# Graph layer kernel: the node stage's result stores are issued by SyncE instead of GpSimd, ahead of the segment loads

## The chip, the cores and the metric

One core of a Trainium2 chip. The metric is the time of one execution on the device, in microseconds; the median of the runs counts.

## The reference

50,000 nodes with 128 features, 50,000 edges sorted by target node, 32 edge types, weights built from 8 bases.

```python
h = jnp.maximum(_layernorm(x, axis=-1), 0.0)
W_rel = jnp.einsum('rb,bdf->rdf', w_comp, weight)
seg = etype * n_nodes + dst
agg = jax.ops.segment_sum(h[src] * norm, seg, num_segments=n_rels * n_nodes)
node_repr = jnp.einsum('rnd,rdf->nf', agg.reshape(n_rels, n_nodes, d_in), W_rel)
node_repr = node_repr + h_bias + h @ loop_weight
x = x + jax.nn.relu(node_repr)
```

## The kernel before

Two stages, all in float32. The *message stage* (up to about 770 us) goes over the edges in 98 groups of 4 tiles of 128 edges: GpSimd gathers rows of `x` by indirect DMA, TensorE multiplies them with all 8 bases, ScalarE and VectorE weigh and add the 8 products, and SyncE stores 4 tiles of messages with their target node to the DRAM tensor `msgs` (L332).

The *node stage* goes over the nodes in 98 groups of 4 windows of 128 nodes (`G` = 4; the last group, 97, has two full windows and one of 80 nodes). Since edges are sorted, the messages of a window are consecutive rows of `msgs`. For a group `g`:

- SyncE (SP) waits for the result of group g - 8, loads four row numbers from `row_tab` (L337) and then loads, for each window, 192 rows of messages into `seg` (L341; 96 partitions of 1032 B). A ring of 8 (`LRING`) holds them.
- GpSimd (POOL) waits for the result of group g - 8, stores it (`store_results`, L491; L493 for the 80 nodes), asks for the rows of `x` of group g into `xw` (`load_x`, L498 and L500; also a ring of 8), and works out `rel` of group g - 3, the place of each message's target in its window (L416), once that group's segments have landed. The rows of `x` and `out` that a partition holds are four rows of 128 numbers, 512 B each, which lie 128 rows apart in DRAM.
- VectorE (DVE) takes statistics of `xw` (L943, L957, L963, L968), makes the one-hot matrices `pick` from `rel` (L932), and makes the result: relu of the sums plus `xw`, into `res` (L1086), a ring of 4 (`NRING`). It waits there until the store of group g - 4 has landed (`n_out`), and counts results in `n_res`.
- ScalarE (ACT) normalises into `hw` (L566) and copies the transposes (L574).
- TensorE (PE) transposes `hw` (L718), and for each window adds three products into PSUM: with `w_loop` (L752), and of `pick` with the two halves of `seg` (L753, L755).

On DVE, the step of group g makes the statistics and `pick` of group g + 1 and the result of group g - 2. The order of work on every engine is written out by hand; all loops are unrolled. A branch for unsorted or crowded targets (`compact > 0`) is not taken with these inputs. The order on SP around the change:

```python
def reload_windows(g, n, q, full=G, last=0):

    sp.wait_ge(n_res, g - (LRING - 1))
    load_windows(g, q, row_tab, n_seg[q], full, last)
```

and on DVE:

```python
if not is_before(g, NRING):

    dve.wait_ge(n_out[r], n * (16 * LRING // NRING) + 16 * (q // NRING))
```

Of the kernel before, what the change touches and what calls it, by code (L numbers as in the profile page):

```python
# [27 lines left out]
P = 128  # L28
G = 4
# [5 lines left out]
NRING = 4  # L35
LRING = 8
# [7 lines left out]
def sweep(eng, count, step, ring=RING, peel=5, first=0):  # L44

    for g in range(first, count):
        step(g, g // ring, g % ring)


def hold(eng, passed):  # L50

    eng.sem_inc(passed, 1)


def round_before(n, q, k=1, ring=RING):

    return n + (q - k) // ring
# [27 lines left out]
def build_layer(nc, x, src, dst_cols, dst, dst_next, type_rows, norm, weight, mix_weight, loop_weight, bias, out):  # L85
    N, D = x.shape
# [6 lines left out]
    NW = -(-N // P)  # L93
    LAST = N - (NW - 1) * P
    NGW = -(-NW // G)
# [16 lines left out]
    with ctx:  # L112
        def sb(name, shape, dt=F32):
            return ctx.enter_context(nc.sbuf_tensor(name, shape, dt))
# [4 lines left out]
        def sem(name):  # L119
            return ctx.enter_context(nc.semaphore(name))  # L120
# [83 lines left out]
        res = sb("res", [P, NRING, G, F])  # L204
# [96 lines left out]
        n_res = sem("n_res")  # L301
        n_out = [sem(f"n_out{q}") for q in range(NRING)]

        X_WIN = x[0:(NW - 1) * P, :].rearrange("(w p) d -> p w d", p=P)
        OUT_WIN = out[0:(NW - 1) * P, :].rearrange("(w p) d -> p w d", p=P)
        LAST_FULL = NW - 1 - (NGW - 1) * G
# [3 lines left out]
        @block.sync  # L310
        def _(sp):

            def load_types(c):
                if c >= 2:
                    sp.wait_ge(s_hot, (c - 1) * TYPES)
                groups = min(TYPES, NG - c * TYPES)
                for j in range(G):
                    sp.dma_start(type_bc[R * j:R * j + R, c % 2, 0:groups, :],
                                 type_rows[j:j + 1, c * TYPES:c * TYPES + groups, :].to_broadcast([R, groups, P])
                                 ).then_inc(s_types[c % 2], 16)  # L320

            sp.dma_start(src_all[:, :], src).then_inc(s_src, 16)
            load_types(0)
            sp.dma_start(norm_all[:, :], norm).then_inc(s_norm, 16)
            sp.dma_start(dst_c[:, :], dst_cols).then_inc(s_dst_c, 16)

            def store_messages(g, n, q):
                if g % TYPES == 0 and (g // TYPES + 1) * TYPES < NG:
                    load_types(g // TYPES + 1)
                sp.wait_ge(s_msg, g * G + G)  # L330
                sp.wait_ge(s_dst_col, g + 1)
                sp.dma_start(msgs[g * G * P:(g + 1) * G * P, :].rearrange("(p t) c -> p (t c)", t=G),  # L332
                             msg[:, q, :, :].rearrange("p t c -> p (t c)")).then_inc(s_stored[q], 16)

            def load_windows(g, q, table, done, full=G, last=0):
                windows = full + (last > 0)
                _, rows = nc.values_load_multi_w_load_instructions(  # L337
                    table[0:1, bass.ds(g * G, windows)], (mybir.EngineType.SP,), min_val=0, max_val=ROWS - SEG,
                    skip_runtime_bounds_check_because="first_row is clamped to EP - SEG or counts compacted rows")
                for j, row in enumerate(rows):  # L340
                    sp.dma_start(seg[0:SEG_P, q, j, :, :].rearrange("p c f -> p (c f)"),  # L341
                                 msgs[bass.ds(row, SEG), :].rearrange("(p c) f -> p (c f)", c=CHUNKS)
                                 ).then_inc(done, 16)

            for g in range(NG):
                store_messages(g, g // RING, g % RING)
                if g == MODE_STORE:
                    sp.wait_ge(s_start, 1)
                    sp.dma_start(mode, mode_i[:, :]).then_inc(s_table, 16)
                if g == NG - PREP:  # L350
                    for q in range(RING):
                        sp.wait_ge(s_stored[q], 16 * 4)
                if 0 <= g - (NG - PREP) < LRING:
                    early = g - (NG - PREP)
                    load_windows(early, early, early_tab, n_seg[early])

            sp.wait_ge(s_table, 16)
            compact = sp.value_load(mode, min_val=0, max_val=1)
            for q in range(RING):
                sp.wait_ge(s_stored[q], 16 * len(range(q, NG, RING)))  # L360

            with sp.If(compact > 0):
                with sp.Fori(0, NW + 2) as w:
                    sp.wait_ge(c_zero, w + 1)
                    hold(sp, passed["sp"])
                    sp.dma_start(msgs[bass.ds(w * P + EP, P), :], cz[:, :]).then_inc(c_zero_st, 16)
                with sp.Fori(0, NT) as t:
                    sp.dma_start(cm[:, :], msgs[bass.ds(t * P, P), :]).then_inc(c_load, 16)
                    sp.wait_ge(c_st, t * 16 + 16)
                    hold(sp, passed["sp"])  # L370


                sp.wait_ge(n_rel, EARLY)
                for q in range(LRING):
                    sp.wait_ge(n_seg[q], 16 * G)
                    load_windows(q, q, row_tab, c_reload)

            def reload_windows(g, n, q, full=G, last=0):

                sp.wait_ge(n_res, g - (LRING - 1))  # L380
                load_windows(g, q, row_tab, n_seg[q], full, last)

            sweep(sp, NGW - 1, reload_windows, LRING, LRING, LRING)
            g = NGW - 1
            reload_windows(g, g // LRING, g % LRING, LAST_FULL, LAST)

        @block.gpsimd
        def _(pool):
# [95 lines left out]
                pool.wait_ge(c_pick, EARLY)  # L484


            def store_results(g, q, full=G, last=0):
                r = q % NRING
                pool.wait_ge(n_res, g + 1)
                if full:  # L490
                    pool.dma_start(OUT_WIN[:, bass.ds(g * G, full), :], res[:, r, 0:full, :]).then_inc(n_out[r], 16)  # L491
                if last:
                    pool.dma_start(out[(NW - 1) * P:N, :], res[0:last, r, full, :]).then_inc(n_out[r], 16)  # L493

            def load_x(g, n, q, full=G, last=0):
                store_results(g - LRING, q)
                if full:
                    pool.dma_start(xw[:, q, 0:full, :], X_WIN[:, bass.ds(g * G, full), :]).then_inc(n_x[q], 16)  # L498
                if last:
                    pool.dma_start(xw[0:last, q, full, :], x[(NW - 1) * P:N, :]).then_inc(n_x[q], 16)  # L500
                window_relative(g - LAG, round_before(n, q, LAG, LRING), (q - LAG) % LRING)
# [3 lines left out]
            def window_relative(g, n, q, windows=G):  # L505
                pool.wait_ge(n_seg[q], n * (16 * G) + 16 * windows)
                if not is_before(g, NRING):
                    pool.wait_ge(n_pick, g - (NRING - 1))
                relative(g, n, q, n_rel, windows)

            for g in range(EARLY, LRING - LAG):
                window_relative(g, 0, g)
            sweep(pool, NGW - 1, load_x, LRING, LRING, LRING)
            last_g = NGW - 1
            load_x(last_g, last_g // LRING, last_g % LRING, LAST_FULL, LAST)
            for g in range(NGW - LRING, last_g):
                ahead = g + LRING - LAG
                if ahead < NGW:
                    window_relative(ahead, ahead // LRING, ahead % LRING, G if ahead < last_g else LAST_FULL + 1)
                store_results(g, g % NRING)  # L520
            store_results(last_g, last_g % NRING, LAST_FULL, LAST)
            for r in range(NRING):
                pool.wait_ge(n_out[r], 16 * (len(range(r, NGW, NRING)) + (r == last_g % NRING and LAST_FULL > 0)))

        @block.scalar
        def _(act):
# [635 lines left out]
```

## Time and profile before

| | |
|---|---|
| median of 3 runs | 1082.01 us (1081.96 to 1083.28) |
| profiled execution, its own time | 1083.85 us |
| its span | 1082.1 us |
| mean granted clock of TensorE | 0.995 of 2.4 GHz |
| busy: PE, DVE, ACT, POOL | 97%, 95%, 86%, 75% |
| DMA queues: GpSimd's (q0) | 28224 packets, 76.93 MB, 26.6% of 16 engines |
| SyncE's (q1) | 59682 packets, 71.69 MB, 22.6% |
| ScalarE's (q10, at the start only) | 1664 packets, 0.82 MB, 0.4% |

The profile is of one execution; its rows are in microseconds from the start of the span. Sizes that it gives as KB are of 1024 B. A DMA's share of an instruction on SP, POOL or ACT is its issue alone; the packets are moved by the core's 16 DMA engines, whose mean busy share has its own row. "To landing" is from issue to the last semaphore update. The windows are in time order: the message stage until about 770 us, then the node stage, whose last loads are issued at about 1055 us.

### The profile page before, as it was taken

The page shows a single profiled execution, that of the slowest core. Times are in us where ns is not written, and L with a number is a line of the kernel's source. Part 1 is how long each engine was busy: PE and PEld are TensorE (multiplying, and loading weights), DVE is VectorE, ACT ScalarE, POOL GpSimd, SP SyncE. Part 2 cuts the span into 40 slices and gives each one's busy share as a digit, 9 for nine tenths or more (in the row PEclk, how much of TensorE's full clock was granted, in tenths as well). Part 3 has the DMA queues.
Part 4 walks back from the last instruction along what each step waited for, and adds up shares of the span by engine and source line. Part 5 has one row for each costly group of instructions (what it writes and reads, how often), then busy time and mean ns, then how long its engine had stood idle before and what let it go on. Part 6 is the DMA issues. An engine that isn't in the chain of part 4 may idle for free. (4 is left out here: it accounts for less than half of the span.)

```text
span 1082.1 us, 23544 instructions
## 1 busy us (share of the span) xinstructions
PE 1047.1 (97%) x4903; PEld 665.9 (62%) x4903; DVE 1024.4 (95%) x4361; ACT 932.3 (86%) x3253; POOL 807.6 (75%) x1381
## 2 busy tenths in 40 slices
PE   1999999999999999999999999999899999999997
PEld 0444444444444444444444444444699999999997
DVE  4999999999999999999999999999899999999995
ACT  6899999999999999999999999998588888888884
POOL 5788888888888888888888888886355555555553
PEclk9999999999999999999999999999899999999999
DMA  6122242224223322322244422222499999999993
GB/s 152 47 77 65 75 109 64 76 72 103 74 67 100 84 65 77 99 76 83 75 119 117 134 75 64 77 66 85 129 294 298 292 301 298 298 298 296 295 299 107
DMA packets 89716, 150.96 MB, mean 140 GB/s; under 512 B 18114, under 2 KB 57346, under 8 KB 89570
## 3 DMA queue, kind: packets, MB, share of 16 engines
q0 software_dynamic: 28224, 76.93, 26.6%
q1 hardware_dynamic: 59682, 71.69, 22.6%
q10 hardware_dynamic: 1664, 0.82, 0.4%
q14 instruction: 106, 0.87, 0.3%
q8 instruction: 40, 0.66, 0.3%
HBM read 97.88 MB, written 51.49 MB: 138 GB/s over the span
## 5 line engine op out<-in xcount | busy, mean ns | idle before, releaser
L687 PE MATMUL y_ps<-w_all,hT 128*128 128x512 f32 x1568 | 691.6, 593 | 2.0 <-DVE sum_a L850 1.8
L687 PEld LDWEIGHTS y_ps<-w_all,hT 128*128 128x128 f32 x1568 | 288.7, 190 | 333.0 <-issue 276.9
L442 POOL DMA_INDIRECT xg<-x,idx x392 | 393.5, 1004 | 77.0 <-issue 49.7
L538 ACT ACTIVATE z<-y_ps,mix 128x128 f32<-128x128 f32 x784 | 244.8, 364 | 61.4 <-PE y_ps L687 47.5
L850 DVE SCALAR_TENSOR_TENSOR sum_b<-y_ps,mix,sum_b 128x128 f32<-128x128 f32 x784 | 265.8, 339 | 0.0
L397 POOL TENSOR_TENSOR u<-z 128x128 f32<-128x128 f32 x392 | 181.6, 463 | 38.1 <-ACT z L538 27.4
L491 POOL DMA_DIRECT2D out<-res x98 | 76.1, 777 | 139.8 <-DVE res L1086 139.8
L566 ACT ACTIVATE hw<-xw,shift,nrstd 128x128 f32<-128x128 f32 x392 | 162.1, 482 | 2.0 <-DVE shift L968 0.5
L752 PE MATMUL y_ps<-w_loop,hwT 128*128 128x128 f32 x782 | 152.1, 276 | 0.0
L753 PE MATMUL y_ps<-seg,pick 96*128 96x128 f32 x782 | 152.0, 275 | 0.0
L755 PE MATMUL y_ps<-seg,pick 97*128 97x128 f32 x782 | 151.8, 275 | 0.0
L850 DVE SCALAR_TENSOR_TENSOR sum_b<-y_ps,mix,z 128x128 f32<-128x128 f32 x392 | 136.0, 347 | 14.6 <-ACT z L534 7.4
L534 ACT ACTIVATE z<-y_ps,mix 128x128 f32<-128x128 f32 x392 | 140.4, 358 | 5.7 <-PE y_ps L687 5.3
L596 ACT ACTIVATE h<-xg,neg_mean 128x128 f32<-128x128 f32 x392 | 135.3, 399 | 0.1
L850 DVE SCALAR_TENSOR_TENSOR sum_a<-y_ps,mix,sum_a 128x128 f32<-128x128 f32 x392 | 133.8, 341 | 1.1 <-DVE sum_b L850 1.0
L850 DVE SCALAR_TENSOR_TENSOR sum_a<-y_ps,mix,u 128x128 f32<-128x128 f32 x392 | 133.8, 341 | 0.8 <-POOL u L397 0.7
L752 PEld LDWEIGHTS y_ps<-w_loop,hwT 128*128 128x128 f32 x782 | 119.2, 192 | 0.5 <-issue 0.5
L753 PEld LDWEIGHTS y_ps<-seg,pick 96*128 96x128 f32 x782 | 119.3, 192 | 0.0
L755 PEld LDWEIGHTS y_ps<-seg,pick 97*128 97x128 f32 x782 | 119.1, 192 | 0.0
L932 DVE TENSOR_TENSOR pick<-iota_n,rel 96x1024 f32<-96x1024 f32 (+1 forms) x100 | 118.0, 1180 | 0.0
L883 DVE TENSOR_TENSOR msg<-sum_a,sum_b 128x128 f32<-128x128 f32 x392 | 114.4, 292 | 0.1
L943 DVE BATCH_NORM_STATS2 nstats<-xw 128x6 f32<-128x128 f32 x392 | 89.9, 275 | 0.0
(94 smaller groups left out, 1204.3 us busy)
## 6 DMA issues: line engine op xcount, KB each, us to landing
seg<-msgs SPq DMA_DIRECT2D x391, 96.8 KB
msgs<-msg SPq DMA_DIRECT2D x98, 258.0 KB
xw<-x POOLq DMA_DIRECT2D x97, 256.0 KB, 5.8
out<-res POOLq DMA_DIRECT2D x97, 256.0 KB, 4.8
type_bc<-type_rows SPq DMA_DIRECT2D x28, 224.0 KB
xg<-x,idx POOLq DMA_INDIRECT x392
w_all<-weight ACTq DMA_DIRECT2D x1, 512.0 KB
dst_i<-dst ACTq DMA_DIRECT2D x1, 196.0 KB, 3.4
```

The lines of the kernel that those rows point to most:

```text
L397: nc.gpsimd.tensor_tensor(u[:, r, :], z[:, r, 0, :], z[:, r, 1, :], ALU.add).then_inc(s_u, 1)
L442: nc.gpsimd.indirect_dma_start(xg[:, q, j, :], None, x, bass.IndirectOffsetOnAxis(ap=idx[:, q, j:j + 1], axis=0)).then_inc(s_gather[q * G ...
L534: nc.scalar.activation(z[:, r, 2, :], y_ps[r][:, B // 2, :], ACT.Copy, scale=mix[:, q, j, B // 2:B // 2 + 1]).then_inc(s_z_high, 1)
L538: ins = nc.scalar.activation(z[:, r, b, :], y_ps[r][:, b, :], ACT.Copy, scale=mix[:, q, j, b:b + 1])
L566: return nc.scalar.activation(hw[:, r, j, :], xw[:, q, j, :], ACT.Relu, bias=shift[:, r, j:j + 1], scale=nrstd[:, r, j:j + 1])
L596: nc.scalar.activation(h[:, q, j, :], xg[:, q, j, :], ACT.Relu, bias=neg_mean[:, q, j:j + 1]).then_inc(s_relu, 1)
L687: nc.tensor.matmul(y_ps[r][:, b0:b0 + B // 2, :], hT[:, q, j, :], w_all[:, b0:b0 + B // 2, :], start=True, stop=True).then_inc(done, 1)
L752: nc.tensor.matmul(y, hwT[:, r, j, :], w_loop[:, :], start=True, stop=False)
L753: nc.tensor.matmul(y, pick[:, r, j, 0, :][0:SEG_P], seg[0:SEG_P, q, j, 0, 0:F], start=False, stop=False)
L755: mm = nc.tensor.matmul(y, pick[:, r, j, 1, :][0:SEG_P + 1], seg[0:SEG_P + 1, q, j, 1, 0:F], start=False, stop=True)
L850: return nc.vector.scalar_tensor_tensor(out=acc, in0=y_ps[r][:, base, :], scalar=c[:, base:base + 1], in1=first, op0=ALU.mult, op1=ALU.add)
L932: return nc.vector.tensor_tensor(pick[0:SEG_P, r, first:windows, :, :].rearrange("p j c n -> p (j c) n"), iota_n[0:SEG_P, :].unsqueeze(1). ...
```

## The change

The stores of `res` go from POOL's program to SP's. For groups 8 to 97 SP now waits for the result of g - 8, stores it and then loads the segments of group g; the last 8 results it stores after all loads, and it waits for the landing of all stores at the end. POOL keeps a wait for the same result ahead of its load of `x`. No size, buffer or amount of data changes.

```diff
--- before.py
+++ after.py
@@ -375,14 +375,26 @@
                     sp.wait_ge(n_seg[q], 16 * G)
                     load_windows(q, q, row_tab, c_reload)
 
+            def store_results(g, q, full=G, last=0):
+                r = q % NRING
+                sp.wait_ge(n_res, g + 1)
+                if full:
+                    sp.dma_start(OUT_WIN[:, bass.ds(g * G, full), :], res[:, r, 0:full, :]).then_inc(n_out[r], 16)
+                if last:
+                    sp.dma_start(out[(NW - 1) * P:N, :], res[0:last, r, full, :]).then_inc(n_out[r], 16)
+
             def reload_windows(g, n, q, full=G, last=0):
-
-                sp.wait_ge(n_res, g - (LRING - 1))
+                store_results(g - LRING, q)
                 load_windows(g, q, row_tab, n_seg[q], full, last)
 
             sweep(sp, NGW - 1, reload_windows, LRING, LRING, LRING)
-            g = NGW - 1
-            reload_windows(g, g // LRING, g % LRING, LAST_FULL, LAST)
+            last_g = NGW - 1
+            reload_windows(last_g, last_g // LRING, last_g % LRING, LAST_FULL, LAST)
+            for g in range(NGW - LRING, last_g):
+                store_results(g, g % NRING)
+            store_results(last_g, last_g % NRING, LAST_FULL, LAST)
+            for r in range(NRING):
+                sp.wait_ge(n_out[r], 16 * (len(range(r, NGW, NRING)) + (r == last_g % NRING and LAST_FULL > 0)))
 
         @block.gpsimd
         def _(pool):
@@ -484,16 +496,8 @@
                 pool.wait_ge(c_pick, EARLY)
 
 
-            def store_results(g, q, full=G, last=0):
-                r = q % NRING
-                pool.wait_ge(n_res, g + 1)
-                if full:
-                    pool.dma_start(OUT_WIN[:, bass.ds(g * G, full), :], res[:, r, 0:full, :]).then_inc(n_out[r], 16)
-                if last:
-                    pool.dma_start(out[(NW - 1) * P:N, :], res[0:last, r, full, :]).then_inc(n_out[r], 16)
-
             def load_x(g, n, q, full=G, last=0):
-                store_results(g - LRING, q)
+                pool.wait_ge(n_res, g - LRING + 1)
                 if full:
                     pool.dma_start(xw[:, q, 0:full, :], X_WIN[:, bass.ds(g * G, full), :]).then_inc(n_x[q], 16)
                 if last:
@@ -517,10 +521,6 @@
                 ahead = g + LRING - LAG
                 if ahead < NGW:
                     window_relative(ahead, ahead // LRING, ahead % LRING, G if ahead < last_g else LAST_FULL + 1)
-                store_results(g, g % NRING)
-            store_results(last_g, last_g % NRING, LAST_FULL, LAST)
-            for r in range(NRING):
-                pool.wait_ge(n_out[r], 16 * (len(range(r, NGW, NRING)) + (r == last_g % NRING and LAST_FULL > 0)))
 
         @block.scalar
         def _(act):
```

SP in the node stage before, one group (`row_tab` holds the row numbers):

```order
L337 TENSOR_LOAD row_tab [waits n_res]
L341 ISA
L341 DMA seg<-msgs 96x258
L341 ISA
L341 DMA seg<-msgs 96x258
L341 ISA
L341 DMA seg<-msgs 96x258
L341 ISA
L341 DMA seg<-msgs 96x258
```

and in the changed kernel:

```order
L382 DMA out<-res 128x4x128 [waits n_res]
L337 TENSOR_LOAD row_tab
L341 ISA
L341 DMA seg<-msgs 96x258
L341 ISA
L341 DMA seg<-msgs 96x258
L341 ISA
L341 DMA seg<-msgs 96x258
L341 ISA
L341 DMA seg<-msgs 96x258
```

The wait for the result has moved from the table load to the store, which stands ahead of the five transfers' other instructions.

POOL in the node stage before, two groups:

```order
L491 DMA out<-res 128x4x128 [waits n_res]
L498 DMA xw<-x 128x4x128
L416 TENSOR_TENSOR rel<-seg,win_off 96x8 [waits n_pick,n_seg5]
L491 DMA out<-res 128x4x128 [waits n_res]
L498 DMA xw<-x 128x4x128
L416 TENSOR_TENSOR rel<-seg,win_off 96x8 [waits n_pick,n_seg6]
```

and in the changed kernel:

```order
L502 DMA xw<-x 128x4x128 [waits n_res]
L428 TENSOR_TENSOR rel<-seg,win_off 96x8 [waits n_pick,n_seg5]
L502 DMA xw<-x 128x4x128 [waits n_res]
L428 TENSOR_TENSOR rel<-seg,win_off 96x8 [waits n_pick,n_seg6]
```

The load of `x` now carries the wait, and follows it directly.

## Rows read from the trace of the kernel before

**Rows 1.** The page, 40 equal slices: DMA share in tenths, GB/s.

```profile
DMA  6122242224223322322244422222499999999993
GB/s 152 47 77 65 75 109 64 76 72 103 74 67 100 84 65 77 99 76 83 75 119 117 134 75 64 77 66 85 129 294 298 292 301 298 298 298 296 295 299 107
```

**Rows 2.** Windows of the node stage: busy us of each engine, then clock, DMA share, GB/s.

```profile
790.00:800.00 10.00, 10.00 (x92) 10.00 (x92) 9.60 (x41) 7.93 (x19) 5.38 (x10) 1.00 1.06 305
...
860.00:900.00 40.00, 40.00 (x362) 40.00 (x361) 38.69 (x153) 32.52 (x78) 23.05 (x39) 1.00 1.04 300
```

**Rows 3.** Waits of 840 to 1060 us (total, times, longest), and POOL's store group.

```profile
POOL out L491 <- DVE res L1086: 92.1, 71, 1.3
...
POOL rel L416 <- DMA seg<-msgs: 0.6, 1, 0.6
...
L491 POOL DMA_DIRECT2D out<-res x71 | 55.3, 779 | 92.1 <-DVE res L1086 92.1
```

**Rows 4.** Timeline of DVE, then POOL, from 949 us: start, duration, instruction, idle before.

```profile
949.41 0.69 DVE L1086 SCALAR_TENSOR_TENSOR res<-y_ps,xw 128x512 f32<-128x512 f32 x1
...
950.93 1.20 DVE L932 TENSOR_TENSOR pick<-iota_n,rel 96x1024 f32<-96x1024 f32 x1
...
952.52 0.69 DVE L1086 SCALAR_TENSOR_TENSOR res<-y_ps,xw 128x512 f32<-128x512 f32 x1
...
950.39 0.78 POOL L491 DMA_DIRECT2D out<-res  x1 [1.31 <-DVE res L1086]
951.17 0.75 POOL L498 DMA_DIRECT2D xw<-x  x1
```

**Rows 5.** SP's own waits of 840 to 1060 us; its segment loads, ns min/median/max.

```profile
SPq L337 <- DVE res L1086: 47.0, 64, 0.8
...
L341 SPq DMA_DIRECT2D seg<-msgs x327: 317/317/1251, 800.9 to 1054.9; - x164
```

**Rows 6.** DMA view of 860 to 1040 us: packets, MB, share of 16 engines; issues, us to landing.

```profile
q0 software_dynamic: 9236, 30.26, 54.3%
q1 hardware_dynamic: 25889, 22.92, 48.4%
...
out<-res POOLq DMA_DIRECT2D x58, 256.0 KB, 5.1
xw<-x POOLq DMA_DIRECT2D x58, 256.0 KB, 5.9
```

**Rows 7.** Windows at the end, 1063 to 1066 us.

```profile
1063.00:1066.00 3.00, 3.00 (x29) 3.00 (x29) 2.90 (x13) 2.42 (x7) 0.65 (x2) 1.00 0.29 87
```

**Rows 8.** DMA view of 830 to 870 us: loads of x, us to landing last.

```profile
xw<-x POOLq DMA_DIRECT2D x13, 256.0 KB, 5.7
```

**Rows 9.** Issues: SP's message stores, ns min/median/max; timeline of ACT's first loads.

```profile
L332 SPq DMA_DIRECT2D msgs<-msg x27: 332/332/363, 204.7 to 399.1; - x27
...
1.66 0.46 ACTq L626 DMA_DIRECT2D w_all<-weight  x1
...
3.62 1.17 ACTq L630 DMA_DIRECT2D seg<-bias  x1
```

**Rows 10.** DMA view of 3 to 8 us, ACT's hardware queue.

```profile
q10 hardware_dynamic: 1089, 0.53, 52.8%
```

**Rows 11.** DMA view of 200 to 400 us, SP's hardware queue.

```profile
q1 hardware_dynamic: 4135, 8.72, 12.8%
```

**Rows 12.** DMA view of 0 to 10 us: GB/s in 40 slices; ACT's queue.

```profile
GB/s 0 0 0 0 0 0 0 157 56 38 194 351 395 378 296 58 86 230 287 344 174 150 258 176 156 158 215 186 270 315 330 348 285 240 244 178 211 268 189 105
...
q10 hardware_dynamic: 1325, 0.73, 39.5%
```

**Rows 13.** Timeline of the end: DVE's last result and POOL's last store; their landing (page).

```profile
1076.17 0.56 DVE L1086 SCALAR_TENSOR_TENSOR res<-y_ps,xw 128x384 f32<-128x384 f32 x1 [1.32 <-PE y_ps L755]
...
1077.71 0.56 POOL L493 DMA_DIRECT2D out<-res  x1
...
out<-res POOLq DMA_DIRECT2D x1, 40.0 KB, 1.9
```

## Prediction

> **What bounds the kernel now.** I read the page first, then the windows by stage, the waits of the node stage, its timeline, and last the DMA view. In the page [rows 1] the last quarter of the span, the node stage, looks different from the rest: the DMA share goes from mostly 2 or 3 tenths to 9 in every slice, at about 298 GB/s. The windows [rows 2] say that PE is busy 40.00 of 40.00 us there at a granted clock of 1.00 and DVE 38.7 of 40, while the DMA share is 1.04, and 1.06 as early as 790 us. PE never waits: the waits of the node stage [rows 3] hold no row of PE and almost none of a DMA (one of 0.6 us). So PE sets the pace, one group of four node windows in 3.12 us (from one result to the next, 949.41 to 952.52 us [rows 4]), and right behind it stand the 16 DMA engines, which have no free time either. That both are full at once is the main fact of this case. POOL has room: it waits 92.1 us in 71 waits for results, 1.3 us in each group [rows 3]. SP waits too: 47.0 us in 64 waits, 0.73 us in each group [rows 5].
>
> **Is the DMA share real load, or packets that wait for each other?** In 860 to 1040 us GpSimd's queue takes 54.3% of 16 engines for 30.26 MB [rows 6]: 0.543 x 16 x 180 us / 30.26 MB = 51.7 us of engine time per MB. One store is 256 KB, 0.262 MB, so 13.6 us over 16 engines, 0.85 us. Near the end, where loads have stopped, one store in 3 us makes a share of 0.29 [rows 7], 0.87 us. The same price alone as in the crowd: the packets are not stretched by waiting, and a share of 1.04 is a DMA system without slack. Its queue does not grow, though: a load of x lands 5.7 us after its issue at 830 to 870 us [rows 8] and 5.9 in the median of 860 to 1040 [rows 6]. So capacity and demand (two transfers of 256 KB and four of 96.8 KB in 3.12 us) are nearly equal now.
>
> **What the change adds and removes, part by part.**
>
> POOL loses 98 store issues, the full ones of 779 ns [rows 3]. The work that covers them is POOL's own waiting, 1.3 us per group; nobody waits for POOL in this stage. Worth nothing by itself. Each x load starts 0.78 us earlier after its result (951.17 becomes about 950.39 [rows 4]), which adds a little lead.
>
> SP gains one store issue per group, ahead of the table load and the four segment loads. Its wait for the result stays where it was, so nothing is queued behind a new wait; what is new is that the segment loads start one issue later. SP's nearest issues take 332 ns (128 rows of 2064 B) and, for a transfer in rows of 512 B, ACT's load of w_all, 0.46 us [rows 9]. I take 0.4 us against the 0.73 us that SP waits now: hidden, with 0.3 us left. If that cover were gone, each us over 0.73 would lengthen every group.
>
> The DMA engines keep the same bytes, but on another queue, which cuts them otherwise. GpSimd's queue moved 30.26 MB in 9236 packets, 3.3 KB each [rows 6], though the rows of out and x are 512 B. The hardware queue of ACT moved w_all, whose rows in memory are also 512 B, in pieces of 487 B on average (1089 packets, 0.53 MB) [rows 10]. So I expect each store as 512 packets of 512 B. Price of a packet on a hardware queue: 0.528 x 16 x 5 us / 1089 = 38.8 ns at 487 B [rows 10]; 0.128 x 16 x 200 us / 4135 = 99.1 ns at 2109 B, SP's message stage [rows 11]. A line through these two gives 53.6 ns at 885 B, and the node stage's own figure for SP's queue is 0.484 x 16 x 180 / 25889 = 53.8 ns at 885 B [rows 6]. The line holds in the crowded stage too, so I take it: 39.7 ns at 512 B, 512 x 39.7 / 16 = 1.27 us per store, against 0.85 us now: **+0.42 us of DMA time per group**.
>
> Its bounds: below, if the store kept long packets, the price per MB of the message stage, 409.6 us / 8.72 MB = 47 us, gives 0.77 us, 0.08 less than now. Above, if the pieces cost what all of the ACT queue cost in its first 10 us, 0.395 x 16 x 10 / 0.73 MB = 87 us per MB [rows 12], 1.42 us, 0.57 more. The line is nearest to what is moved, since it is supported by a row at either side of 512 B and by one of this stage.
>
> The page "DMA: Bandwidth & Descriptors" of the Trainium skill, section "Why small descriptors are slow (HBM only)", has a smaller price for it: about 3 cycles more for each packet of 32-byte beats. As an estimate by it, eight packets of 512 B take 152 cycles where one of 4096 B takes 131, 16% more, +0.14 us per store; the sum below would then end at +4 us, 1086. The rows above speak for the larger figure.
>
> **The sum.** The DMA engines are full from 790 us [rows 2] to about 1055, where the page's last full slice ends [rows 1], 265 / 3.12 = 85 groups. 85 x 0.42 = 35.7 us more DMA time. Not all of it reaches PE at once, since transfers have a lead: a store lands about 5.1 us after its issue [rows 6], at 950.39 + 5.1 = 955.5, and its buffer is written again four groups later, at 949.41 + 12.5 = 961.9 [rows 4]. 6.5 us, say 7, are eaten up before DVE's next result waits for a store, and PE for DVE; the segment loads have some 8 us by the same count (their picks start five groups less 1.6 us after the result that let them go). At the end the last result is done at 1076.73, and POOL issues two stores after it, the second at 1077.71 for 0.56 us; that one, landing 1.9 us after its issue, ends the kernel [rows 13]. SP would take about 0.35 us for each and start the first earlier, so the second would be issued some 0.7 us and done 0.9 us earlier: -1 us. Together 35.7 - 7 - 1 = **+28 us**. The profiled execution took 1083.85 us, which is 1.8 us over the median of the runs; from 1082.0, the median, I get **1110 us**.
>
> **The rivals.**
>
> *No change (1081 us).* The engines are the same 16; if a store on SP costs no more than about 0.1 us of them over what it costs now (85 x 0.1 = 8.5 us, about the lead of 7 us plus the 1 us at the end), nothing reaches PE, and the gain at the end alone is left, 1 us. For it: PE has no wait at all today, the queue doesn't grow, single slices reach 344 to 395 GB/s in the first 10 us [rows 12], so an engine can go faster than 298. Against it: the share of 1.04, the price of a lone store, and the packets of 512 B on ACT's queue. It decides at the packet's price: under 30 ns (0.96 us per store), this case; above, mine. That is the one on the other side.
> The same page of the Trainium skill, section "Issuing engines are not separate DMA queues", says that transfers issued by any engine run on the same DMA engines, so that another issuer saves only issue time; by that rule the time stays at 1081 to 1082. The one fact it leaves out here, and which the rows show, is that the two kinds of queue cut the same rows into packets of another size.
>
> *SP becomes the bound (about 1111 us for an issue of 1.17 us).* Behind w_all's 1024 pieces ACT's small issues got longer, up to 1.17 us for a load of 16 KB [rows 9]: the queue holds the issuer back. If SP's group cost 1.17 us more, 0.44 over its 0.73 of waiting, 85 x 0.44 = 37 less 8 gives +29 us. For it: those rows, and single segment loads of up to 1.25 us [rows 5]. Against: SP's median stays 317 ns, and the store is half of w_all. The profile would show SP without any wait for results and DMA under 1.0.
>
> *Faster by over 0.2%.* It would need PE or DVE faster in the stage or more than 2.2 us at the end. Nothing in the rows does this, but for a load of x that starts 0.78 us earlier, for which nobody waits.
>
> **How the numbers follow.** 0.2%, 2.2 us, is about what a measurement of this kernel can tell. My forecast 0.57, SP as the bound 0.08, no change 0.31, faster 0.04. Slower by over 0.2%: 0.57 + 0.08 = 0.65; within: 0.31; faster: 0.04. My own case alone spans from 0.14 us per store (85 x 0.14 - 8 = +4, 1086) to 0.57 (48.5 - 8 = +40, 1122). The range must take in the case of no change: 1081. At the top SP and DMA can both be dear, which I allow 6 us: 1128.
>
> **What would show it.** Right: the hardware queue's packets rise by some 50,000 with 512 B each, and its share in the node stage by more than GpSimd's falls; the period goes from 3.12 to about 3.5 us, not in the first 15 to 20 groups but after the lead is used; DVE's result (or pick) then waits for a DMA of SP's queue, PE shows short gaps; POOL waits about 2 us per group. Wrong in price: packets of 2 KB or more, or 512 B at under 30 ns. Wrong in the bound: packets as dear as said, a share well over 1.1 and PE still busy without a gap, which would mean that the share of before was stretched after all.

## The result and the profile after

The changed kernel takes 1079.84 us (median of 20 runs, 1078.61 to 1080.91), the one before 1082.44 (20 runs, 1081.89 to 1084.13): a ratio of 0.9973, 95% interval 0.9966 to 0.9980, 2.6 us less. The prediction was +28 us. It had the wrong sign, and the measured time lies outside its range. (A few executions of the experiments took 1236 to 6324 us, far from their fellows; the medians and ratios below are without them.)

The profiled execution of the change took 1078.61 us with a span of 1076.8. Its windows of the node stage, which answer to [rows 2] (busy us of PE, PEld, DVE, ACT, POOL, then clock, DMA share, GB/s):

```profile
800.00:850.00 50.00, 50.00 (x451) 50.00 (x450) 48.38 (x196) 40.68 (x96) 27.61 (x32) 1.00 1.08 296
...
900.00:950.00 50.00, 50.00 (x451) 50.00 (x450) 48.28 (x193) 40.74 (x97) 27.74 (x32) 1.00 1.11 298
```

The DMA view of 860 to 1040 us, against [rows 6] (packets, MB, share of 16 engines; KB each and us to landing):

```profile
q1 hardware_dynamic: 55427, 37.41, 79.3%
q0 software_dynamic: 4628, 15.18, 29.4%
...
seg<-msgs SPq DMA_DIRECT2D x230, 96.8 KB, 4.5
xw<-x POOLq DMA_DIRECT2D x58, 256.0 KB, 6.7
out<-res SPq DMA_DIRECT2D x58, 256.0 KB, 7.1
```

The waits of 840 to 1060 us on the engines, against [rows 3] (total, times, longest):

```profile
POOL xw L502 <- DVE res L1086: 90.6, 68, 2.0
...
POOL rel L428 <- DMA seg<-msgs: 21.8, 24, 2.9
```

and SP's own, against [rows 5]:

```profile
SPq L382 <- DVE res L1086: 6.9, 5, 2.7
```

Half of the picture is the predicted one. Stores go in short packets (29,538 more in this window), a store lands after 7.1 us instead of 5.1, and the DMA share is up to 1.11. But PE is busy 50.00 of 50 us. SP has almost no wait left: 6.9 us where it had 47.0. POOL waits 21.8 us for segments, from which PE sees nothing.

Where the time went is read from the result instructions (`res`, L1086) of the two timelines, first the kernel before, then the change (start, duration):

```profile
771.94 0.65 DVE L1086 SCALAR_TENSOR_TENSOR res<-y_ps,xw 128x512 f32<-128x512 f32 x1
777.88 0.69 DVE L1086 SCALAR_TENSOR_TENSOR res<-y_ps,xw 128x512 f32<-128x512 f32 x1 [2.95 <-PE y_ps L755]
```

```profile
770.33 0.65 DVE L1086 SCALAR_TENSOR_TENSOR res<-y_ps,xw 128x512 f32<-128x512 f32 x1
775.38 0.69 DVE L1086 SCALAR_TENSOR_TENSOR res<-y_ps,xw 128x512 f32<-128x512 f32 x1 [2.06 <-PE y_ps L755]
...
1073.65 0.56 DVE L1086 SCALAR_TENSOR_TENSOR res<-y_ps,xw 128x384 f32<-128x384 f32 x1 [1.32 <-PE y_ps L755]
```

The end of the second result to the end of the last is 776.07 to 1074.21, 298.14 us, in the change, and 778.57 to 1076.73 [rows 13], 298.16 us, before: the stage itself is the same to 0.02 us. From the last result to the end of the span (1082.07 and 1076.76 us with two decimals) it is 5.34 us before and 2.55 us after: 2.8 us, as much as the whole difference of the medians. (The profiled executions differ by 2.5 us more, ahead of the second result: 1.6 us up to the first result and 0.9 us from there to the second. In the twelve profiled executions without a late start, those of both kernels and ten of the experiments, the first result began at 770.3 to 771.9 us and the second 4.7 to 5.9 us later, with either kind of store, so this is scatter.)

What makes the end shorter stands at the instructions put down to line L112, among them the last of each engine. Before:

```profile
L112 DVEq DRAIN  x1: 597/597/597, 1076.2 to 1076.2; - x1
...
L112 POOLq DRAIN  x1: 2031/2031/2031, 1079.8 to 1079.8; - x1
```

and in the change:

```profile
L112 POOLq DRAIN  x1: 2368/2368/2368, 1059.3 to 1059.3; - x1
...
L112 SPq DRAIN  x1: 13/13/13, 1076.5 to 1076.5; - x1
```

(ns min/median/max, then first and last start.) Each engine has a DRAIN instruction at the end of its program. GpSimd's took 2.03 us and stood behind its wait for the last store, so nothing covered it; in the change it lies at 1059 us, beside the rest of the stage, and SP's takes 13 ns.

### The profile page after: what moved, and what is told of

The parts are those of the page before. It is cut to its first block, busy times and chain, and to the rows that moved or that the text cites. A ratio compares the mean times of both kernels' runs of the same rounds, so it can differ in the third digit from the quotient of the medians.

```text
span 1076.8 us, 23544 instructions
## 1 busy us (share of the span) xinstructions
PE 1046.8 (97%) x4903; PEld 665.2 (62%) x4903; DVE 1024.1 (95%) x4361; ACT 932.3 (87%) x3253; POOL 782.7 (73%) x1282
## 4 chain that ended last, share of the span: by engine, by line
PE 95%; DVE 2%; DMA 1%; ACT 1%; issue 0%; POOL 0%; DVEq 0%; ACTq 0%
PE y_ps L687 61%; PE y_ps L752 8%; PE y_ps L755 8%; PE y_ps L753 8%; PE hT_ps L707 4%; PE hT_ps L718 2%; PE mix_ps L718 2%; PE mix_ps L703 1%; DMA xg<-x,idx 1%; DVE sum_a L850 0%; DVE sum_b L850 0%; POOL xg L454 0%; DMA src_all<-src 0%; PE y_ps L673 0%; DVE pick L932 0%
## 5 line engine op out<-in xcount | busy, mean ns | idle before, releaser
L502 POOL DMA_DIRECT2D xw<-x x90 | 69.3, 770 | 127.1 <-DVE res L1086 127.1
L428 POOL TENSOR_TENSOR rel<-seg,win_off 96x8 f32<-96x8 f32 x98 | 75.9, 776 | 23.5 <-DMA seg<-msgs 21.8
```

## The experiments

The runs were made in three sets, each beside its own runs of the kernel before (1082.57, 1082.42 and 1082.30 us). Ratios are to that kernel, with a 95% interval. Each diff shows the lines that matter; semaphores that are only declared, and waits whose counts follow, are left out.

### The end alone, the stage alone

**tail_sp.** From the kernel before, only the last 8 stores go to SyncE; they count on semaphores of their own, and VectorE's waits for them follow.

```diff
@@ sync, after the last reload_windows
+            for g in range(NGW - LRING, last_g):
+                store_last(g)
+            store_last(last_g, LAST_FULL, LAST)
+            for r in range(NRING):
+                sp.wait_ge(n_out[r], 16 * len(range(r, NGW - LRING, NRING)))
+                sp.wait_ge(n_last[r], 32 + 16 * (r == (NGW - 1) % NRING and LAST_FULL > 0))
@@ gpsimd
-                store_results(g, g % NRING)
-            store_results(last_g, last_g % NRING, LAST_FULL, LAST)
-            for r in range(NRING):
-                pool.wait_ge(n_out[r], 16 * (len(range(r, NGW, NRING)) + (r == last_g % NRING and LAST_FULL > 0)))
```

> Only the last 8 stores are SyncE's; the 90 of the stage stay GpSimd's. Theory T (the gain is at the kernel's end: GpSimd's DRAIN of 2.03 us after its last wait goes, and two store issues of 0.71 and 0.56 us become 0.37 and 0.47): 2.6 to 2.8 us less than before, about 1079.7, with the last result to the end of the span 2.5 us instead of 5.3. Rival S (the stage itself gains, by x loads that start 0.8 us earlier): 1 to 2 us less gain than the full change, 1081 or more.

1080.12 us, ratio 0.9976 (0.9967 to 0.9985), 2.5 us less. Last result to end of span: 1077.5 - 1074.83 = 2.7 us. This is the change's gain, with the stage left alone.

**stage_sp.** The complement: the changed kernel with its last 8 stores, and the last wait, back on GpSimd.

```diff
@@ sync
-            for g in range(NGW - LRING, last_g):
-                store_results(g, g % NRING)
-            store_results(last_g, last_g % NRING, LAST_FULL, LAST)
-            for r in range(NRING):
-                sp.wait_ge(n_out[r], 16 * (len(range(r, NGW, NRING)) + (r == last_g % NRING and LAST_FULL > 0)))
@@ gpsimd
+                store_last(g)
+            store_last(last_g, LAST_FULL, LAST)
```

> The 90 stores of the stage are SyncE's, the last 8 GpSimd's again. T: the same as before within 0.3 us, 1082.4, since PE sets the period of 3.12 us in both, and the end is as before, 5.3 us from the last result. S: 1 us or more of the gain stays, 1081.4 or less. The theory of the prediction (DMA time) would have put the loss here: there is none if the period stays 3.12 us.

1083.33 us, ratio 1.0009 (1.0000 to 1.0017): 0.8 us more than before, not less, and more than the 0.3 us that the expectation allowed. Its stage is 298.13 us long, so the excess is not there; in the profiled execution the end is 5.8 us instead of 5.3. GpSimd issues its last two stores 0.5 us later after the last result (1076.16 - 1075.37 = 0.8 us instead of 1077.02 - 1076.73 = 0.3 us) and starts its DRAIN 0.9 us later, 1.55 us long this time. Why the issue is late was not tried. SP waits 0.4 us in all of 840 to 1060 us and PE still never waits. The 90 stores of the stage bring nothing; theory T stands and S falls.

**pool_wait.** The change, with the last wait on GpSimd.

```diff
@@ sync
-            for r in range(NRING):
-                sp.wait_ge(n_out[r], 16 * (len(range(r, NGW, NRING)) + (r == last_g % NRING and LAST_FULL > 0)))
@@ gpsimd, at the end
+            for r in range(NRING):
+                pool.wait_ge(n_out[r], 16 * (len(range(r, NGW, NRING)) + (r == last_g % NRING and LAST_FULL > 0)))
```

> The change with one thing put back: GpSimd instead of SyncE waits at the end until all stores have landed. T1 (a DRAIN of GpSimd costs some 2 us wherever it stands): 1.9 to 2.1 us more than the change, 1081.8. T2 (the DRAIN was long only because GpSimd had just issued the stores itself): under 0.3 us more than the change, 1080.

1082.23 us, ratio 0.9998 (0.9989 to 1.0007): 2.3 us more than the change if each is set against the median before of its own set, 2.7 us by the ratios, and 2.1 us by the profiled executions (last result to end 1078.97 - 1074.31 = 4.66 us against 2.55). Its DRAIN rows:

```profile
L112 SPq DRAIN  x1: 127/127/127, 1075.3 to 1075.3; - x1
L112 POOLq DRAIN  x1: 2112/2112/2112, 1076.6 to 1076.6; - x1
```

GpSimd had issued its last transfer more than 20 us before, and its DRAIN still takes 2.11 us. T1 is right and T2 falls: one wait on the wrong engine costs 2.1 of the 2.8 us that the end became shorter. The other 0.7 us (5.34 - 4.66) stay, with the stores on SyncE.

**wait_sp.** The kernel before, with only that wait moved to SyncE.

```diff
@@ sync, after the last reload_windows
+            for r in range(NRING):
+                sp.wait_ge(n_out[r], 16 * (len(range(r, NGW, NRING)) + (r == last_g % NRING and LAST_FULL > 0)))
@@ gpsimd, at the end
-            for r in range(NRING):
-                pool.wait_ge(n_out[r], 16 * (len(range(r, NGW, NRING)) + (r == last_g % NRING and LAST_FULL > 0)))
```

> The kernel before with only its last wait moved: SyncE waits until all stores have landed, GpSimd still issues them all. T1 (GpSimd's DRAIN costs about 2 us wherever it stands): it runs beside the landing of 1.9 us, and the end comes 1.5 to 1.9 us earlier, 1080.6 to 1081.0. Rival: the DRAIN holds until GpSimd's own transfers have landed and then takes its 2 us, no gain, 1082.5.

1081.50 us, ratio 0.9989 (0.9979 to 0.9998): 0.8 us less by the medians, 1.2 us by the ratio and by the end of the profiled execution (1078.9 - 1074.78 = 4.1 us). That is less than T1's 1.5 to 1.9:

```profile
L112 POOLq DRAIN  x1: 3137/3137/3137, 1075.5 to 1075.5; - x1
...
L112 SPq DRAIN  x1: 13/13/13, 1077.9 to 1077.9; - x1
```

SP is done at 1077.9, GpSimd's DRAIN only at 1078.6, 2.3 us after the end of its last issue (1075.77 + 0.56). A DRAIN beside the landing is partly hidden, and here still ends last.

**tail_sp_act.** tail_sp, with the store of the last 80 nodes on ScalarE.

```diff
@@ sync, store_last
-                if last:
-                    sp.dma_start(out[(NW - 1) * P:N, :], res[0:last, r, full, :]).then_inc(n_last[r], 16)
@@ scalar, at the end
+            act.wait_ge(n_res, NGW)
+            act.dma_start(out[(NW - 1) * P:N, :], res[0:LAST, (NGW - 1) % NRING, LAST_FULL, :]).then_inc(n_last[(NGW - 1) % NRING], 16)
```

> As tail_sp, but the very last store, 80 nodes, is issued by ScalarE while SyncE issues the one of two windows. T: the two issues of 0.37 and 0.47 us run side by side, 0.4 us less than tail_sp, about 1079.3. Rival: the landing of the first store ends last anyway, no difference.

1080.46 us, ratio 0.9978 (0.9968 to 0.9988), no better than tail_sp; last result to end 2.8 us. The gain of 0.4 us did not come: the 40 KB landed 2.1 us after the start of ScalarE's issue, where they took 1.6 us after SP's in tail_sp, so both kernels have all stores landed 2.0 to 2.1 us after the last result.

### How much room the DMA engines had

**extra64.** The kernel before, with one more store of 64 KB per group on GpSimd's queue; GpSimd also waits for all of them at its end.

```diff
+    scratch = nc.dram_tensor("scratch", [(NGW - LRING) * 1 * P, F], F32, kind="Internal").ap()
@@ gpsimd
             pool.wait_ge(s_src, 16)
+            pool.wait_ge(s_weights, 16 * 4)
@@ load_x
+                pool.dma_start(scratch[(g - LRING) * 1 * P:(g - LRING + 1) * 1 * P, :].rearrange("(w p) d -> p w d", p=P), w_all[:, 0:1, :]).then_inc(s_extra, 16)
```

> The kernel before with one more store per group on GpSimd's queue, 64 KB of constant data to a scratch tensor, in 90 groups: 0.21 us of DMA time per group. Theory F (the DMA engines were full at a share of 1.04, as the prediction had it): 85 x 0.21 = 18 less 8 us of lead, 10 us slower, 1092. Theory R (there was room in a share of 1.04, the packets get shorter when more wait): no change, 1082 to 1083, share about 1.08 to 1.1, over 310 GB/s.

1092.45 us, ratio 1.0094 (1.0077 to 1.0111): 10.0 us more, exactly what theory F expected. The agreement is an accident. The result rows of its timeline:

```profile
785.15 0.69 DVE L1091 SCALAR_TENSOR_TENSOR res<-y_ps,xw 128x512 f32<-128x512 f32 x1 [2.80 <-PE y_ps L760]
...
1083.42 0.56 DVE L1091 SCALAR_TENSOR_TENSOR res<-y_ps,xw 128x384 f32<-128x384 f32 x1 [1.32 <-PE y_ps L760]
```

The stage runs from 785.84 to 1083.98, 298.14 us, not a tenth longer; all of it starts 7 us later (778.57 before) and its end is 1 us longer (6.3 us). The late start comes from the wait for the weights that the edit put at GpSimd's start, and which holds back the first gathers; extra64b, without it, starts on time.

**extra64b.** The same, with that wait moved to just ahead of the node stage.

```diff
@@ gpsimd
-            pool.wait_ge(s_weights, 16 * 4)
@@ after the first window_relative calls
+            pool.wait_ge(s_weights, 16 * 4)
```

> extra64 without what disturbed it: the wait for the source of the extra stores stands now ahead of the node stage instead of at GpSimd's start, where it had delayed the first gathers by some 8 us. Theory R (room in the DMA engines): no change against before in the stage, 298.1 us from the second to the last result, and 1082 to 1083 in all. F: 1092 again.

1083.76 us, ratio 1.0014 (1.0005 to 1.0023): 1.5 us more in all, with an unchanged stage (777.57 to 1075.70 us, 298.13) and a longer end (6.3 us instead of 5.3, of which 0.9 us is GpSimd's DRAIN, 2.93 us instead of 2.03). Windows 860 to 1040 us of it:

```profile
860.00:1040.00 180.00, 180.00 (x1619) 180.00 (x1618) 174.13 (x695) 146.66 (x347) 131.66 (x232) 1.00 1.05 317
```

against 1.04 and 297 GB/s in the same window of the kernel before. 7% more bytes at nearly the same share: a share of 1.04 was not a full DMA system. F falls. The time of a packet is no fixed price either: SP's queue, with the same packets, has a share of 43.7% in this window instead of 48.4%, 0.437 x 16 x 180 us / 25,818 = 48.7 ns each instead of 53.8, as theory R had it.

**extra128.** 128 KB per group (`scratch` twice as large, `w_all[:, 0:2, :]`), otherwise as extra64, with its late start.

> The same with 128 KB per group, 0.42 us of DMA time: the size of cost that the prediction gave the change. F: 85 x 0.42 = 36 less 8, 28 us slower, 1110. R: no change or a few us; 337 GB/s would be moved in the stage if the period stays 3.12 us.

1098.4 us, ratio 1.0162 (1.0138 to 1.0185). The stage takes 304.57 us, 6.4 more; the other 10 us lie outside it, most in the same late start. The window:

```profile
860.00:1040.00 180.00, 175.43 (x1565) 174.27 (x1565) 168.80 (x678) 141.10 (x337) 136.44 (x226) 1.00 1.05 328
```

Here transfers are the bound, at 328 GB/s, and the share is still 1.05. The waits of 840 to 1060 us show it: GpSimd waits 24.4 us for segments, though SyncE, which loads them, still has 47.5 us of waiting for results and issued them in time. Whether the DMA engines themselves or the memory behind them give out at 328 GB/s was not tried. As an estimate, with 0.42 us more per group (half of a store's 0.85), 85 groups and 8 us of lead, 6.4 us of loss mean a room of 0.42 - 14.4 / 85 = 0.25 us per group in the kernel before. It takes packet times as fixed, which extra64b shows they are not, so it is good for the order of size. The first gap in PE's pace comes after 25 groups, as a lead that is used up would have it.

**after_extra64.** The changed kernel with extra64b's edit.

> The changed kernel with the same 64 KB more per group on GpSimd's queue, 0.21 us of DMA time. If the change used 0.12 us of a room of about 0.3 us per group, this goes over it by little: R: 0 to 6 us slower than the change, first stall late. If SyncE's held-up issues grow with the load of the engines (its group takes 3.13 us of 3.12 already): 5 to 15 us slower, with SyncE never waiting. No change at all would say that both have more room than I think.

1082.71 us, ratio to the kernel before 1.0010 (0.9994 to 1.0025): 3.0 us over the change if each is set against its own median before, 4.0 us by the ratios. The runs lie between 1081.17 and 1088.74 us. In the profiled one (1084.09 us) the stage is 302.90 us, 4.8 more, at 308 GB/s, with the first gap after 50 groups. The kernel before bears the same 64 KB without a gap (extra64b), so the change has used a part of the room. As an estimate by the same reckoning, DMA time per group rose by (79.3 + 29.4 - 54.3 - 48.4)% x 180 us / 57.7 groups = 0.19 us; with 0.21 more it is 0.15 over the 0.25, 85 x 0.15 = 13 less 8 of lead: 5 us. SP's waits in it are 6.5 us, as few as in the change, so whether the engines or SP's issues make those 4.8 us is not separated.

### What holds SyncE

**split_sp.** The change, each store cut in two.

```diff
-                if full:
-                    sp.dma_start(OUT_WIN[:, bass.ds(g * G, full), :], res[:, r, 0:full, :]).then_inc(n_out[r], 16)
+                for f in range(0, full, 2):
+                    sp.dma_start(OUT_WIN[:, bass.ds(g * G + f, 2), :], res[:, r, f:f + 2, :]).then_inc(n_out[r], 16)
```

> The change with each store on SyncE cut into two of two windows: the same bytes and 512-byte packets, one issue of 0.42 us and some 0.1 us around it more per group. Theory Q (SyncE's issue time is the next bound: its group costs 2.9 us plus held-up issues now, and it waits only 6.9 us in the stage): about 3.35 us per group against 3.12, 90 x 0.23 = 21 us behind at the end of the loads, of which the lead hides some 8 to 12: 9 to 13 us slower than the change, 1089 to 1093. Rival D (the DMA engines are what holds SyncE up): within 1 us of the change, since no packet changes.

1137.77 us, ratio 1.0510 (1.0492 to 1.0528): 58 us more than the change, far over the 9 to 13 expected. The kind of bound is that of theory Q:

```profile
860.00:1040.00 180.00, 156.32 (x1312) 152.74 (x1311) 139.52 (x561) 115.66 (x282) 45.50 (x92) 0.96 0.89 239
```

The DMA share falls to 0.89 while PE stands still 24 us of 180, and SP waits 0.2 us in 840 to 1060. A piece of its timeline (start, length, issues):

```profile
901.76 0.94 SPq L382 DMA_DIRECT2D out<-res  x2
903.34 1.94 SPq L341 DMA_DIRECT2D seg<-msgs  x4
905.62 0.92 SPq L382 DMA_DIRECT2D out<-res  x2
907.29 1.90 SPq L341 DMA_DIRECT2D seg<-msgs  x4
909.24 0.93 SPq L382 DMA_DIRECT2D out<-res  x2
```

A group takes SP 3.86 and 3.62 us here, 180 / 46 = 3.9 in the mean, 0.8 more than the change's 3.12. The second issue is 0.46 + 0.05 us of it. The load of the row numbers behind it has a median of 501 ns instead of 302, and single issues are held up for over a microsecond. The size missed because I took SP's group as 2.9 us plus a little; it was already 3.12.

**split_pool.** The same cut on GpSimd, in the kernel before (`pool.dma_start` in the diff above).

> The kernel before with GpSimd's stores cut in two in the same way: one issue of about 0.75 us more per group against 1.3 us that GpSimd waits. Both theories: no change in the stage, 1082 to 1083. Only if DMA time per transfer mattered would it be slower.

1083.84 us, ratio 1.0012 (1.0003 to 1.0022); stage 298.13 us, POOL's wait for results 44.0 us instead of 92.1, and the end longer, 6.5 us, with a DRAIN of 3.17 us. An issue that GpSimd has time for costs nothing in the stage. So what split_sp loses, it loses on SyncE's side, and not by the number of transfers as such.

**store2k.** The change with its 90 stage stores going to a scratch tensor in rows of 2048 B; the rows of `out` of groups 0 to 89 are not written.

```diff
+    scratch = nc.dram_tensor("scratch", [(NGW - LRING) * P, G * F], F32, kind="Internal").ap()
@@ store_results
-                if full:
+                if full and g < NGW - LRING:
+                    sp.dma_start(scratch[g * P:(g + 1) * P, :], res[:, r, :, :].rearrange("p w d -> p (w d)")).then_inc(n_out[r], 16)
+                elif full:
```

> The change with the 90 stores of the stage going to a scratch tensor in which a partition's four rows lie together, so that a store is 128 pieces of 2048 B instead of 512 of 512 B; the rows of out of groups 0 to 89 are left unwritten. If the number of pieces is what lifts the DMA share and holds SyncE up: share back to 1.02 to 1.04, the segment loads' mean issue back from 380 to about 340 ns, SyncE waits for results again, some 0.2 to 0.3 us per group. If it is the bytes on its queue: SyncE waits as little as in the change. The time is the change's either way, within 1 us.

1079.93 us, ratio 0.9978 (0.9966 to 0.9989), the change's time. In 860 to 1040 us:

```profile
q1 hardware_dynamic: 34018, 37.90, 75.5%
q0 software_dynamic: 4626, 15.17, 28.4%
```

21,400 packets fewer than in the change for 1% more bytes, and the two shares add to 103.9% against 108.7: the short packets are what lifts the DMA share. But SP waits 5.0 us in 840 to 1060, no more than in the change, and the mean of its segment issues, over the trace's records of 860 to 1040 us, is 377 ns against 380 in the change and 338 before. So the held-up issues do not come with the number of packets, and that half of the expectation fell. They come with the store on SP's queue, be it by its bytes or as one transfer more per group; these two were not separated, nor was it tried what exactly holds an issue back.

## Why the prediction was wrong

**"The same price alone as in the crowd: the packets are not stretched ... a DMA system without slack" failed, and carried the forecast.** The price is real for GpSimd's stores, 0.85 us per store in a crowd and 0.87 alone. But I took the sum of packet times over 16 engines for how full they are. extra64b moved 317 GB/s at 1.05 and extra128 328 at 1.05: from 297 to 328 GB/s the share hardly moves, while bytes per unit of share rise, and the change itself runs at 1.09 without a gap in PE. The room was, by the estimate from extra128, 0.25 us per group. The row that spoke for it was in the text, under the rival: PE without a single wait, a queue that didn't grow. A queue that never builds up in 85 groups says "not full" more surely than any share.

**The price of a packet was mis-sized.** 39.7 ns at 512 B came from a line through 487 and 2109 B. Measured: (0.793 - 0.484) x 16 x 180 us / 29,538 packets = 30.1 ns, 0.96 us per store instead of 1.27. (Counted by size in the traces, a packet of 512 B took 30.6 ns in the mean there, and SP's packets of 1032 B took 61.5 ns against 61.0 before, so the rise is the stores' own.) The line's lower end was w_all's load at the kernel's start, where the engines fetch many things at once, and its figure at 885 B is a mean over packets of 1032 B and very small ones; that the two met proved nothing for 512. The traces had a stretch with lone stores, 1060 to 1074 us, where only stores of `res` are moved. First SP's in the change, then GpSimd's before:

```profile
q1 hardware_dynamic: 2536, 1.26, 29.1%
```

```profile
q0 software_dynamic: 343, 1.14, 27.0%
```

That is 0.291 x 16 x 14 us / 1.26 MB = 51.7 us per MB on SP's queue and 53.1 on GpSimd's, 0.85 and 0.87 us for a store: alone, the short packets (25.7 ns each) cost nothing more at all. Only in traffic do they get dearer, which the prediction had ruled out from the times of GpSimd's long packets. That stores would be cut into 512 packets was right, and that this costs DMA time there too: +0.11 us for the store and +0.07 for the load of x beside it (55.8 us per MB instead of 51.7), +0.19 us per group in all. The estimate of +0.14 us per store by the Trainium skill's page "DMA: Bandwidth & Descriptors", section "Why small descriptors are slow (HBM only)", was nearer than mine of 0.42; the traces put 0.11 beside it in traffic, and nothing alone.

With both sizes put right the same sum gives 0.19 under a room of about 0.25: nothing in the stage, as measured. The prediction named its own turning point, 30 ns per packet, and the measured price lies on it. With no room at all, 85 x 0.19 = 16 us less 8 of lead would still have been a loss of 8 us, so it is the room that decided.

**The lead** of 7 to 8 us held as an order of size: extra128's first gap came after 25 groups, 25 x (0.42 - 0.25) = 4 us, and after_extra64's after 50, 50 x 0.15 = 7.5 us.

**SP, "0.4 us against 0.73: hidden, with 0.3 us left", came out right only in its result.** The store's issue takes 0.46 us in the mean and 0.1 us around it, and the four segment issues, 380 ns each in the mean instead of 338, take 0.17 us more. All 0.73 us are used; from 860 to 1040 us SP never waits, and its group takes 3.12 us. The rival "SP becomes the bound" had 0.08 and was the nearest danger: split_sp falls over that edge with one more issue.

**POOL** as predicted in size, worth nothing in the stage: stage_sp shows it.

**The end: -1 us predicted, -2.8 measured.** From the last result on I counted issues and landing only. SP's two issues of 0.37 and 0.47 us and an earlier start give some 0.9 us, as said; the rest is GpSimd's DRAIN, 2.03 us, which no row in my list showed, though 2.5 us lay unexplained between the landing at 1079.6 and the end of the span at 1082.1. The section "Issuing engines are not separate DMA queues" of the same page of the Trainium skill lets another issuer save only issue time. The stage agrees, 298.14 us against 298.16; the end does not, since 2.0 of its 2.8 us are GpSimd's DRAIN. The rival "faster", at 0.04, asked for over 2.2 us at the end, and that is where it was.

## What to carry to other kernels

A DMA share of about 1 is no measure of fullness: look whether anything waits for a transfer and whether landing times grow, and add a known amount of traffic if it matters. Take a price for packets from packets of that size on that kind of queue, alone and in traffic. Let the engine with the shortest DRAIN, here SyncE, issue the last stores and wait for them, and let GpSimd finish early. Moving the stage's stores as well brought nothing here and used up SyncE's spare time; tail_sp has the whole gain with SyncE's waits kept (44.9 us). Once an experiment moves the total by the expected amount, check that it did so in the stretch that was meant: extra64 agreed with a wrong theory to a tenth of a microsecond, and the timeline's result rows undid it.

## What the runs showed of the hardware

- The DRAIN at the end of GpSimd's program took 1.55 to 3.53 us in the 14 kernels traced, 2.11 us where its last transfer was issued more than 20 us before; SyncE's took 13 to 133 ns. What sets GpSimd's length within this range stays open.
- Packets of 512 B on SyncE's hardware queue took 30.1 ns each in a total traffic of 294 GB/s and 25.7 ns alone. Per MB alone that is 51.7 us, against 53.1 for GpSimd's packets of the same stores.
- The DMA engines moved 297, 317 and 328 GB/s at shares of 1.04, 1.05 and 1.05 in the same window of the stage, the last with PE held up; the change moved 294 GB/s at 1.09 with PE never idle.
- With a store of 256 KB more per group on its queue, SyncE's issues of unchanged transfers became longer, from 338 to 380 ns in the mean, with packets of 512 B and of 2048 B alike.
